# A software pipeline over 32 rounds in which a normalisation chain, two bank releases and five TensorE blocks change places

## What is computed

```python
# attn_a: gated linear attention, 16 heads, dk 8, dv 16, then an MLP 256-512-256
h = _ln(x, ln_w, ln_b)
S = jnp.exp(gt)[..., None] * S + kt[..., None] * vt[..., None, :]   # for each time step
o = einsum('bhk,bhkv->bhv', qt, S)
x = x + (_rms(o, rms_w) * (g * sigmoid(g))) @ Wo
x = x + gelu(_ln(x) @ W1 + b1) @ W2 + b2
...
# attn_b: recurrence with a state of 16
h = jnp.tanh(xb_t + h @ A.T)                                        # for each time step
y = (h @ C) @ W_out.T + b_out
...
# ffn: 8 experts of 256x256, the two best of each token (a mixture; run twice)
out = ((combined + remap_bias) * weights).sum(axis=0)
...
x = x + attn_a(_layernorm(x))
x = x + ffn(_layernorm(x))      # mixture 1
x = x + attn_b(_layernorm(x))
x = x + ffn(_layernorm(x))      # mixture 2, same weights
```

## Time and profile before

| | us |
|---|---|
| median of three runs | 1695.19 |
| lowest, highest | 1692.84, 1696.77 |
| profiled execution, time | 1698.78 |
| its span | 1696.7 |

### The profile page before, as it was taken

How to read it: one execution, slowest core, us unless ns; L and a number is a source line. 1 busy time by engine, 2 the same in 40 slices (tenths; PEclk the granted TensorE clock), 3 DMA queues, 4 the chain that set the end, 5 groups by cost and what they waited for, 6 DMA issues and landing times.

```text
span 1696.7 us, 51149 instructions
## 1 busy us (share of the span) xinstructions
PE 1585.6 (93%) x16584; PEld 1331.2 (78%) x16584; DVE 1267.8 (75%) x4557; ACT 1035.8 (61%) x3852; POOL 822.9 (49%) x1293
## 2 busy tenths in 40 slices
PE   4688999999999999999999999999999999998866
PEld 3577788888888888888888888888888888887654
DVE  4566777887788778787877887788778877776644
ACT  4655666666666666666666666766666666655431
POOL 3554454554555455545454554554555545543211
PEclk8798999999999999999999999999999999999978
DMA  5211112111111111011111111111111111110000
GB/s 154 80 57 45 52 57 57 42 39 43 43 56 56 56 51 42 31 51 48 56 56 56 44 36 43 44 55 56 56 54 42 40 43 43 52 51 8 7 6 13
DMA packets 117121, 81.48 MB, mean 48 GB/s; under 512 B 41888, under 2 KB 108096, under 8 KB 116928
## 3 DMA queue, kind: packets, MB, share of 16 engines
q1 hardware_dynamic: 116080, 80.10, 15.6%
q10 hardware_dynamic: 976, 0.54, 0.1%
HBM read 47.06 MB, written 33.55 MB: 48 GB/s over the span
## 4 chain that ended last, share of the span: by engine, by line
PE 60%; issue 12%; POOL 9%; DVE 9%; DMA 5%; SPq 2%; ACT 2%; POOLq 0%; DVEq 0%; ACTq 0%
PE ps L1253 50%; DMA xag<-in_x 3%; PE ps L1270 2%; PE ps L1259 2%; DVE acc L892 2%; DVE hs L860 1%; DMA arow<-att 1%; POOL r L402 1%; PE ps L1299 1%; PE ps L1440 1%; SPq L314 1%; DVE att L949 1%; PE ps L1319 1%; PE ps L1310 1%; POOL res L495 1%
## 5 line engine op out<-in xcount | busy, mean ns | idle before, releaser
L1253 PE MATMUL ps<-we,yT 128*128 128x512 f32 x3072 | 826.7, 411 | 11.5 <-DVE mv_f L879 11.0
L1253 PEld LDWEIGHTS ps<-we,yT 128*128 128x128 f32 x3072 | 539.5, 190 | 117.8 <-DVE mv_f L879 19.5
L566 ACT ACTIVATE h_lead<-ps 48x8 fp32r<-48x8 f32 x1024 | 171.6, 168 | 487.9 <-PE ps L1270 474.1
L860 DVE SCALAR_TENSOR_TENSOR hs<-ps,cst,h_lead 48x8 fp32r<-48x8 f32 x1024 | 224.6, 219 | 249.7 <-ACT ps L567 244.9
L1270 PEld LDWEIGHTS ps<-hs,aT 128*128 128x128 f32 x1024 | 195.1, 191 | 104.9 <-DVE hs L860 73.7
L1270 PE MATMUL ps<-hs,aT 128*128 128x8 f32 x1024 | 208.8, 204 | 42.5 <-DVE hs L860 40.5
L892 DVE SCALAR_TENSOR_TENSOR stage<-ps,coef,stage 128x256 f32<-128x256 f32 x384 | 182.8, 476 | 13.9 <-POOL stage L432 5.6
L892 DVE SCALAR_TENSOR_TENSOR acc<-ps,coef,acc 128x256 f32<-128x256 f32 x384 | 181.8, 474 | 9.3 <-POOL acc L432 4.2
L517 POOL TENSOR_TENSOR orstd<-omean,mhalf 128x32 f32<-128x32 f32 x32 | 174.8, 5461 | 0.2
L567 ACT ACTIVATE ps<-ps 48x8 f32<-48x8 f32 x1024 | 163.1, 159 | 0.0
L430 POOL TENSOR_TENSOR part<-part 128x256 f32<-128x256 f32 x64 | 47.2, 737 | 218.4 <-ACT part L584 216.0
(11 more groups left out here) (185 smaller groups left out, 3197.7 us busy)
## 6 DMA issues: line engine op xcount, KB each, us to landing
arow<-att SPq DMA_DIRECT2D x32, 512.0 KB, 2.8
atx<-arow SPq DMA_DIRECT2D x128, 128.0 KB, 2.8
vrow<-vtok SPq DMA_DIRECT2D x32, 256.0 KB, 2.1
vx<-vrow SPq DMA_DIRECT2D x128, 64.0 KB, 2.0
out<-stage SPq DMA_DIRECT2D x64, 128.0 KB
xin<-in_x SPq DMA_DIRECT2D x62, 128.0 KB
xag<-in_x SPq DMA_DIRECT2D x62, 128.0 KB
stage<-in_experts SPq DMA_DIRECT2D x1, 2048.0 KB, 10.0
```

Of the source, the lines that this page charges most:

```text
L566: a.activation(h_lead[:], ps[0:NB, BANK["RB"], k * B:(k + 1) * B], ACT.Tanh)
L860: v.scalar_tensor_tensor(hs[0:NB, :, k], h_whole, keeps_rest, h_lead[:].bitcast(F32), ALU.mult, ALU.subtract).then_inc(sem("rnn_h"), 1)
L1253: ins = t.matmul(dst, left(lp, c), right(rp, c), start=(n == 0), stop=(n == 3 * chunks - 1))
```

## The change

The edits of the diff, in its order:
- `BANK_ORDER`: F2's bank is free when `x1` is there, no longer at `mv_m1`; WO's at `xmid`, no longer at `mv_f`. The waits of G2_7 and G1_0 on TensorE change with it.
- GpSimd: `rstd` of m1 stands ahead of that of m2.
- ScalarE: the first half of mixture 2's normalisation moves from between the tanh pairs of steps 4 and 5 to behind that of step 7.
- VectorE: `split_state(2)` and `split_state(3)` each move ahead, of the addition of F2 and of the `stats` behind it; `split_state(16)` moves ahead of a combination of mixture 1.
- TensorE: the scores of both tiles stand together ahead of step 2, with F2's second tile behind it; the first two of six matmuls of G2_7 move ahead of step 4, the other four stay behind step 5; read_state and state_update stand together behind step 4.

```diff
-    6: [("F1B", 4, ("gT", FB, 4)), ("QK", 2, 'qt'), ("KT", 2, 'ktok'), ("F2", 4, 'mv_m1'),
+    6: [("F1B", 4, ("gT", FB, 4)), ("QK", 2, 'qt'), ("KT", 2, 'ktok'), ("F2", 4, 'x1'),
...
-    7: [("G2_2", 7, ("acc2", 2 * VECTOR_GROUPS, 4)), ("OG", 3, 'oTs'), ("WO", 3, 'mv_f'),
+    7: [("G2_2", 7, ("acc2", 2 * VECTOR_GROUPS, 4)), ("OG", 3, 'oTs'), ("WO", 3, 'xmid'),
...
@@ ScalarE
-                if live(it, 7):
-                    act.wait_ge(sem("shift_m2"), c7)
-                    normed(m2.y, m2.x, m2.r, 0).then_inc(sem("ym2"), 1)
                 if live(it, 6):
                     state_of(5, c6)
...
                 if live(it, 6):
                     state_of(7, c6)
+                if live(it, 7):
+                    act.wait_ge(sem("shift_m2"), c7)
+                    normed(m2.y, m2.x, m2.r, 0).then_inc(sem("ym2"), 1)
                 if live(it, 7):
                     normed(m2.y, m2.x, m2.r, 1).then_inc(sem("ym2"), 1)
@@ VectorE
+                if live(it, 5):
+                    split_state(16, c5)
                 if live(it, 4):
                     dve.wait_ge(sem("moe1"), past((c4 - 1) * GROUPS + 3))
                     combine(m1, 2, 0, BANK["G1_2"], c4)
-                if live(it, 5):
-                    split_state(16, c5)
@@ TensorE
                     scores(0)
+                if live(it, 2):
+                    scores(1)
+                if live(it, 5):
+                    step(2, c5)
                 if live(it, 4):
                     ins = product(ps[:, BANK["F2"], 1 * D:2 * D], lambda p, f: gTs[:, p, f, 1 * P:2 * P],
                                   lambda p, f: wcols(W_2, p, f, D, 0, D), FB)
...
+                if live(it, 7):
+                    for name, count in readers(it, "G2_7"):
+                        pe.wait_ge(sem(name), count)
+                    moe(m2, 7, BANK["G2_7"], 0, 2)
+                if live(it, 5):
+                    step(4, c5)
                 if live(it, 2):
                     read_state(0)
                     read_state(1)
-                if live(it, 5):
-                    step(4, c5)
...
                 if live(it, 7):
-                    for name, count in readers(it, "G2_7"):
-                        pe.wait_ge(sem(name), count)
-                    moe(m2, 7, BANK["G2_7"]).then_inc(sem("moe2"), 1)
+                    moe(m2, 7, BANK["G2_7"], 2).then_inc(sem("moe2"), 1)
```

More of the change, by code:

```diff
@@ L471, in body @@
                     inner_rstd(c1)
+                if live(it, 4):
+                    target = value(pool, c4)
+                    pool.wait_ge(sem("pads_zero"), 1)
+                    pool.wait_ge(sem("mv_m1"), target)
+                    rstd(m1.mv, m1.r, "m1", c4, True)
                 if live(it, 6):
@@ L476, in body @@
                     rstd(m2.mv, m2.r, "m2", c6, True)
-                if live(it, 4):
-                    target = value(pool, c4)
-                    pool.wait_ge(sem("pads_zero"), 1)
-                    pool.wait_ge(sem("mv_m1"), target)
-                    rstd(m1.mv, m1.r, "m1", c4, True)
                 if live(it, 3):
@@ L1048, in body @@
                     moments(m2.st, m2.mv, "m2", c6)
+                if live(it, 5):
+                    split_state(2, c5)
                 if live(it, 4):
@@ L1053, in body @@
                 if live(it, 5):
-                    split_state(2, c5)
+                    split_state(3, c5)
                 if live(it, 4):
@@ L1057, in body @@
                     stats(m1.x, m1.st, "m1")
-                if live(it, 5):
-                    split_state(3, c5)
                 if live(it, 4):
@@ L1474, in body @@
                 if live(it, 5):
-                    step(2, c5)
-                if live(it, 2):
-                    scores(1)
+                    step(3, c5)
                 if live(it, 3):
@@ L1484, in body @@
                                   lambda p, c: wcols(W_O, p, c, D, 0, D), KC)
+                if live(it, 7):
+                    for name, count in readers(it, "G2_7"):
+                        pe.wait_ge(sem(name), count)
+                    moe(m2, 7, BANK["G2_7"], 0, 2)
                 if live(it, 5):
-                    step(3, c5)
+                    step(4, c5)
                 if live(it, 2):
```

## The result

| | before | changed |
|---|---|---|
| median, us | 1697.05 (6 runs) | 1730.24 (1726.93 to 1731.45, 6 runs) |
| profiled execution: span | 1696.7 | 1729.5 |
| iteration, median of the inner 26 | 48.66 | 49.87 |

The account below looks back on a forecast made before the run. Bound by TensorE's program order; a 1.68 us GpSimd lag costs TensorE 1.18 us an iteration, less 0.10 for split_state(16): 1.08, 29.2 us over 27 iterations plus 1.0, 30.2 on 1695.2, so 1725.5 us; range 1706 to 1745.

Follow-up runs that it names:

- lag_1: The kernel before plus one 128x256 addition on GpSimd ahead of `rf`, its result unused: 1696.84 us, 0.9992.
- lag_2: The kernel before plus two 128x256 additions on GpSimd ahead of `rf`, their results unused: 1709.77 us, 1.0062.
- the early load: The kernel before with the sync engine's second load of x issued ahead of its wait for `att_out`, nothing else: 1691.68 us, 0.9952.
- the kernel with the blocks: The changed kernel with GpSimd's order and ScalarE's move undone: 1.0028; with the second load of x issued ahead of the `att_out` wait, 0.9975.
- the kernel without them: The kernel before with both bank releases and the `split_state(16)` move: 0.9970; with x's second load issued ahead of the `att_out` wait, 0.9930.

## What to carry to other kernels

When a short chain is put ahead of another on an in-order engine, ask first when its input is there: if it was not waiting before, putting it ahead only makes all that stands behind it late. Then measure the room: a useless instruction of known length at the same place (lag_1, lag_2) gives it in two runs, if the lag is read from the trace and not from the number of instructions. When an edit seems to give a loss back, make the same edit where the loss is not: the early load gave the kernel with the blocks 0.53%, and the kernel without them 0.40%. And look at what stands behind a wait in the queue of the DMA-issuing engine too: here one load, issued ahead of a wait it had no need of, was worth as much as both bank releases.
